# Layer 1 of the last batches behind layer 0 of the last batch, in a two-layer cross-attention kernel

## The reference

```python
x = x + _L0_xattn_ref(_layernorm(x), ctx_512, ...)   # causal self attention + cross attention, 16 heads of 16
x = x + _L0_ffn_ref(_layernorm(x), w1, b1, w2, b2)   # per-token int8 inputs, ternary weights, exact gelu
x = x + _L1_xattn_ref(_layernorm(x), ctx_512, ctx_512, ...)  # cross attention, 16 heads
x = x + _L1_ffn_ref(_layernorm(x), w1, b1, w2, b2)   # int8 with ONE scale over all batches
```

## Time and profile before

| | us |
|---|---|
| median of 3 runs | 1926.49 (1925.32 to 1931.07) |
| the profiled execution | 1921.53 |
| its span, first to last instruction | 1919.7 |
| PE busy in the span | 1685.9 |
| DVE busy | 1370.9 |
| ACT busy | 1156.6 |
| POOL busy | 659.1 |
| mean granted TensorE clock | 0.946 |

### The profile page before, as it was taken

The page is one execution under the profiler, slowest core; times in us unless marked ns, Lnnn a source line. Parts: engine busy times, 40 slices in busy tenths (PEclk is TensorE's granted clock), DMA queues, the critical chain, the costliest instruction groups (busy, mean ns, idle before and its releaser), DMA issues.

```text
span 1919.7 us, 29141 instructions
## 1 busy us (share of the span) xinstructions
PE 1685.9 (88%) x10052; PEld 732.4 (38%) x10064; DVE 1370.9 (71%) x2549; ACT 1156.6 (60%) x2178; POOL 659.1 (34%) x915
## 2 busy tenths in 40 slices
PE   4898889997999899998999899998999899678677
PEld 1344334423543344333542344333542354241236
DVE  6667767777687767777777758876777768638376
ACT  1374475566755585657655675567556676552597
POOL 3332523541454134522355044522354041140040
PEclk7898999999999999999999999999999999796998
DMA  7334313332242323331332324231333223014023
GB/s 198 88 104 127 89 34 95 83 93 69 60 110 63 85 67 93 84 97 56 94 87 73 86 56 115 75 90 56 95 84 86 59 56 96 0 52 147 23 88 111
DMA packets 106947, 159.49 MB, mean 83 GB/s; under 512 B 20656, under 2 KB 83248, under 8 KB 106800
## 3 DMA queue, kind: packets, MB, share of 16 engines
q1 hardware_dynamic: 101904, 156.43, 29.5%
...
## 4 chain that ended last, share of the span: by engine, by line
PE 54%; DVE 25%; ACT 10%; POOL 4%; issue 4%; DMA 1%; ACTq 0%; SPq 0%; DVEq 0%; POOLq 0%
DVE nmax L1222 13%; PE acc L1459 13%; PE mx L1424 11%; PE st L1445 9%; PE misc L1399 6%; PE misc L1371 4%; PE misc L1486 3%; PE misc L1411 3%; ACT probs L965 3%; ACT tail_h L1035 2%; DVE hid L1176 2%; ACT tail_h L1020 1%; ACT hid L1000 1%; PE misc L1513 1%; ACT hqT L924 1%
## 5 line engine op out<-in xcount | busy, mean ns | idle before, releaser
L1222 DVE TENSOR_REDUCE nmax<-mx 128x1 f32<-128x512 f32 (+2 forms) x1376 | 872.2, 673 | 318.4 <-PE mx L1424 189.5
L965 ACT ACTIVATE probs<-st 128x512 f32<-128x512 f32 (+3 forms) x1536 | 764.2, 549 | 410.4 <-PE st L1445 261.4
L1424 PE MATMUL mx<-stack 96*128 96x512 bf16 (+3 forms) x1536 | 550.8, 371 | 124.0 <-DVE nmax L1222 100.0
L1445 PE MATMUL st<-stack 99*128 99x512 bf16 (+3 forms) x1536 | 542.7, 366 | 28.8 <-ACT probs L965 27.3
L1424 PEld LDWEIGHTS mx<-stack 96*128 96x128 bf16 x1536 | 151.5, 99 | 355.1 <-DVE nmax L1222 281.3
L1445 PEld LDWEIGHTS st<-stack 99*128 99x128 bf16 x1536 | 149.6, 99 | 355.6 <-ACT probs L965 196.5
L844 POOL TENSOR_TENSOR parts<-qk,zero 128x512 bf16<-128x512 f32 x78 | 81.2, 1041 | 211.7 <-ACT qk L948 211.7
L1459 PE MATMUL acc<-probs,v_x 128*32 128x512 f32 x1024 | 145.9, 644 | 0.0
L1459 PE MATMUL acc<-probs,v_f 128*32 128x512 f32 x1024 | 140.0, 619 | 0.4 <-ACT probs L965 0.3
L856 POOL TENSOR_TENSOR nparts<-nmax,zero 128x16 bf16<-128x16 f32 x96 | 21.3, 222 | 287.0 <-DVE nmax L1222 287.0
L1448 PE MATMUL st<-mask_st,identb 128*128 128x128 bf16 x512 | 111.7, 221 | 0.0
...
## 6 DMA issues: line engine op xcount, KB each, us to landing
...
```

What stands on the lines that cost most here:

```text
L965: act.activation(probs[:, j % P_SLOTS, c, T - w:], st_bank(n, 4 * j + c)[:, 0:w], ACT.Exp, scale=SCALE).then_inc(exp_done, 1)
L1222: dve.tensor_reduce(nmax[:, ring, first:first + NT * (len(cs) - 1) + 1:NT], src, AX.X, ALU.max, negate=True).then_inc(mx_free, 1)
L1424: last = pe.matmul(o, stack[0:ROWS, r, 0, c, P * i:P * i + P], stack[0:ROWS, r, 1, c, 0:w], start=True, stop=not causal)
L1445: last = pe.matmul(o[:, 0:w], stack[0:AUG, r, 1, c, P * j:P * j + P], stack[0:AUG, r, 0, c, T - w:T], start=True, stop=not causal)
```

## The change

The same steps, 4374 in all, in another order from the start of x6_0 on:

```diff
-ORDER = [u for b in range(B + 1) for u in turn_units(b)]
+LATE = [(b, p) for b in (B - 2, B - 1) for p in "xs"] + [(b, "f") for b in (B - 3, B - 2, B - 1)]
+ORDER = [u for b in range(B - 2) for u in turn_units(b)] + [u for b, p in LATE for u in units(b, p)]
...
+def late_turns():
+    a, b, c = B - 3, B - 2, B - 1
+    keys_c, queries_c = project_qk(c, "f")[:2 * 4], project_qk(c, "f")[2 * 4:]
+    norm_c = [x for x in layer1_norm(c) if x != ("ctx_T", c, "C")]
+    f = units(c, "f")
+    first, second = ([("maxima", u, k) for k in banks_of(u)] for u in f[:2])
+    return [("load1", a), ("load0", c)] + \
+        slots(units(b, "x") + units(b, "s")[:1], [None] * 6 + [("y_T", a - 1, "C")] +
+              blend(ffn_main(a, [("residual", a - 1, "C"), ("v", b, "s")], layer1_last(a - 1)), tokens0(c) + project_qk(c, "x")) +
+              [("v", c, "x")], B) + \
+        slots(units(b, "s")[1:], [("load_mid", b)] + project_qk(c, "s") + layer1_norm(a) + [("v", a, "f"), None] + project_qk(a, "f"), B) + \
+        slots(units(c, "x")[:1], [None] * 6 + layer0_end(b) + [("load1", b)], B) + \
+        slots(units(c, "x")[1:] + units(c, "s"), ffn_norm(b) + ffn_main(b, [("v", c, "s")]) + [("load_mid", c)] +
+              layer1_norm(b) + [("v", b, "f"), None] + project_qk(b, "f"), B) + \
+        slots(units(a, "f")[:1], [None] * 6 + layer0_end(c) + [("load1", c)], B) + \
+        slots(units(a, "f")[1:], ffn_norm(c) + [("ctx_T", c, "C")] + blend(ffn_main(c, [("v", c, "f")]), keys_c), B - 1) + \
+        slots(units(b, "f")[:1], [None] * 3 + norm_c + queries_c, B - 1) + \
+        slots(units(b, "f")[1:2], [("stack", f[0])] + layer1_end(a) + [("stack", f[1])], B - 1) + \
+        slots(units(b, "f")[2:], first + [("negmax", f[0]), ("stack", f[2])] +
+              second[:9] + [("negmax_T", f[0])] + second[9:], B - 1) + \
+        slots(f[:1], [None] * 6 + layer1_end(b), B) + slots(f[1:], [], B) + close(f[-1]) + layer1_end(c)
```

As three batches now wait for layer 1 at once, their data get other buffers, and a few waits are added:

```diff
         def x1_of(s):
-            return y["s"] if last_batch(s) else x1
+            return {B - 2: ctx_all["A"][:, :].rearrange("p (t c) -> p t c", c=C), B - 1: y["s"]}.get(batch(s), x1)
         def xn_of(s, k):
-            return xn["A"] if k == "C" and last_batch(s) else xn[k]
+            return {("C", B - 2): xn["A"], ("E", B - 2): xn["A"], ("C", B - 1): xmid}.get((k, batch(s)), xn[k])
+        def y_of(s, p):
+            return {("f", B - 2): xn["A"], ("f", B - 1): y["x"]}.get((p, batch(s)), y[p])
+        def v_of(s, p):
+            return v_aug[{("f", B - 2): "x", ("f", B - 1): "s"}.get((p, batch(s)), p)]
+        def parts_of(b, w):
+            return qk_parts["x" + w[1] if (w[0], b) == ("f", B - 2) else w]
...
-            last_read("down", B - 1, NT - 1)
+            last_read("norm_T", B - 1, "C")
+            sp.wait_ge(peak, 2 * (B - 1))
             sp.wait_ge(stored, 32 * B)
...
+                if k == "C" and s.key[1] == B - 2:
+                    for m in range(KC):
+                        wait_misc_read(dve, s, m, ("norm_T", B - 1, "A"))
+                if k == "E" and last_batch(s):
+                    dve.wait_ge(stored, 32 * (B - 1))
...
+                    elif s.key[1] == B - 2:
+                        for m in range(KC):
+                            wait_misc_read(dve, s, 0, ("project", B - 1, "xk", m))
+                        for k in range(2):
+                            wait_misc_read(dve, s, k, ("v", B - 1, "x"))
...
                 if s.unit == (B - 1, "f", 0):
-                    dve.wait_ge(stored, 32 * B)
+                    dve.wait_ge(y_summed, B + 1)
```

More of the change, by code:

```diff
@@ L66, in turn_units, with units @@
     return layer0 + layer1
-ORDER = [u for b in range(B + 1) for u in turn_units(b)]
+def units(b, p):
+    return [(b, p, g) for g in range(NU)]
+LATE = [(b, p) for b in (B - 2, B - 1) for p in "xs"] + [(b, "f") for b in (B - 3, B - 2, B - 1)]
+ORDER = [u for b in range(B - 2) for u in turn_units(b)] + [u for b, p in LATE for u in units(b, p)]
 AT = {u: n for n, u in enumerate(ORDER)}
@@ L252, in turn @@
             slots(us[5:8], [("v", 1, "x"), ("load_mid", 0)] + weights([2, 3]) + project_qk(1, "s"), 1)
-    more = b + 1 < B
-    loads = [("load1", b - 1)] + ([("load0", b + 1)] if more else [])
+    loads = [("load1", b - 1), ("load0", b + 1)]
     if b == 1:
@@ L259, in turn @@
         start = slots(us[:5], [None] * 6 + [("y_T", b - 2, "C")] +
-                      ffn_main(b - 1, [("residual", b - 2, "C"), ("v", b, "s")], layer1_last(b - 2)) + layer1_start(b - 1), b + more)
-    if not more:
-        return loads + start + slots(us[5:6], [("load_mid", b)], b) + slots(us[6:8], [], b) + \
-            slots(us[8:9], [None] * 6 + layer0_end(b), b) + \
-            slots(us[9:12], layer0_ffn(b) + [("load1", b)] + layer1_norm(b) + project_qk(b, "f"), b)
-    return loads + start + \
-        slots(us[5:6], [("load_mid", b)] + (tokens0(b + 1) if more else []), b + more) + \
-        slots(us[6:8], project(b + 1, "x") if more else [], b + more) + \
-        slots(us[8:9], [None] * 6 + layer0_end(b), b + more) + \
-        slots(us[9:12], blend(ffn_norm(b), project_qk(b + 1, "s")), b + more)
+                      ffn_main(b - 1, [("residual", b - 2, "C"), ("v", b, "s")], layer1_last(b - 2)) + layer1_start(b - 1), b + 1)
@@ new lines, in turn @@
+    return loads + start + \
+        slots(us[5:6], [("load_mid", b)] + tokens0(b + 1), b + 1) + \
+        slots(us[6:8], project(b + 1, "x"), b + 1) + \
+        slots(us[8:9], [None] * 6 + layer0_end(b), b + 1) + \
+        slots(us[9:12], blend(ffn_norm(b), project_qk(b + 1, "s")), b + 1)
+def late_turns():
[19 more added lines that the diff above has]
+        slots(f[:1], [None] * 6 + layer1_end(b), B) + slots(f[1:], [], B) + close(f[-1]) + layer1_end(c)
@@ L275 @@
     warm_up(FIRST)[3:] + [("consts_rest", 0)]
-AFTER = close((B - 2, "f", NU - 1)) + warm_up(turn_units(B))[:3] + layer1_end(B - 2) + [("v", B - 1, "f")] + \
-    warm_up(turn_units(B))[3:] + slots(turn_units(B), [], B, True) + close((B - 1, "f", NU - 1)) + layer1_end(B - 1)
 TURNS = [[s for s in steps if s] for steps in
-         [BEFORE + turn(0) + turn(1)] + [turn(b) for b in range(2, B - 1)] + [turn(B - 1) + AFTER]]
+         [BEFORE + turn(0) + turn(1)] + [turn(b) for b in range(2, B - 2)] + [late_turns()]]
 RING_USES = {
@@ L306, in shifted @@
     return (s[0], later) + s[2:]
-for t in range(1, B - 3):
-    assert [shifted(s) for s in TURNS[t]] == TURNS[t + 1], "the loop's turns differ"
 RING_PER_TURN = {r: START[TURNS[2][0]][r] - START[TURNS[1][0]][r] for r in RING_USES}
@@ L1458, in values @@
                 for c in range(HU):
-                    last = pe.matmul(acc[32 * c:32 * c + 32, T - w:T], v_aug[p][:, j, HU * g + c, :],
+                    last = pe.matmul(acc[32 * c:32 * c + 32, T - w:T], v_of(s, p)[:, j, HU * g + c, :],
                                      probs[:, j % P_SLOTS, c, T - w:T], start=j == 0, stop=j == NT - 1)
```

24 lines of the change are left out of this document (14 added, 10 removed).

## The result

The changed kernel takes **1910.55 us** (median of 4, 1909.33 to 1911.45) where the kernel before took 1925.9 beside it: ratio 0.9916, 95% interval [0.9897, 0.9935]. The interval leaves out 1, so it is faster, by 15 us or 0.8%. The forecast was 1886.0 with a range of 1872 to 1905: the sign was right, the size was not, and the range didn't reach the result. The profiled execution took 1909.82 us with a span of 1908.0.

The account below looks back on a forecast made before the run. It took TensorE's work to bound a steady turn. Pieces priced mostly in TensorE time summed to 458.7 us for the 499.2 us reordered stretch, 40.5 less, giving 1886.0 us for the median, range 1872 to 1905.

Parts of the forecast that it names:

- The bubble: From the start of f6_3 to f7_0, 61.8 us with TensorE busy 45.7, because f7 needs all of batch 7's layer 0.
- (b): Rival at batch 7's layer-1 start: keys and queries still late, the 12.4 us chain comes back bare; 1898 us, chance 0.05.
- (c): Rival where projections bunch (s6_1, s6_3, s7_3): maxima splits queue on GpSimd and TensorE waits, 53 us; 1939 us, chance 0.03.
- (d): Rival: idle time only moves and nothing is gained, 1.6 us more in each of 25 units; chance 0.03.
- The loads for the last FFN: Issued in f7_1, beside the maxima rows of f7_2 and f7_3: bounds 0 to 3 us, taken as 0.
- The pieces x6_0 to s6_3: Cross-attention and causal units of batch 6: 99.9 us for x6_0 to s6_0, 51.0 for s6_1 to s6_3.
- `layer1_end` at 4.7 us: End of layer 1, in f6_1 and f7_0: priced in TensorE time from turn 6 at 4.7 us each.
- The quantisation and the gelu, 12.5 us each time: Layer-0 FFN in x7_1 to x7_3 and f5_1 to f5_3: quantisation 4.5 us, gelu 8.0, beyond their matmuls.
- rival (a): Late gelu blocks cost what f6_1 and f6_2 did, 19.8 us instead of 12.5, twice, 14.6 more; 1901 us, chance 0.14.
- x7_0 and f5_0: First units of batch 7's cross-attention and batch 5's layer 1, each priced at 16.8 us as f5_0 before.
- second way of counting: Check on the reordered stretch: TensorE's 432.2 us busy less 18 us of lower clock, over 0.924, gives 448 us.
- TensorE busy over 90% of the stretch: Sign of a right forecast: TensorE busy over 90% from 1270 to the start of f7_1.

Follow-up runs that it names:

- experiment 9: The changed kernel once more, with no edit, as a base for later runs: median 1911.53 us, ratio 0.9922 to the kernel before.
- Experiments 3: Changed kernel with 3.6 us more TensorE work in batch 5's layer-1 end and 3.6 us more VectorE work in batch 6's: 1916.37 us.
- experiment 4: Changed kernel with layer 1's last statistics, norm, peak and store of batches 5 and 6 moved behind the start of f7_2: 1902.49 us, ratio 0.9871.
- experiment 11: Changed kernel with layer 1's last part moved, GpSimd's addition held until after quantisation, and scale and quantisation spread among maxima: 1894.66 us, ratio 0.9832.
- after: The changed kernel as first measured and profiled, against the kernel before: median 1910.55 us, profiled execution 1909.82, ratio 0.9916.
- experiment 5: Changed kernel with GpSimd's row addition of batches 6 and 7 waiting until VectorE has made the quantised copy: 1907.78 us.
- Experiment 2: Changed kernel with each split of the layer-1 projections made four list entries of one VectorE operation, maxima between: 1909.14 us.

## Why the prediction was wrong, point by point

**Right.** The bubble is gone, and the rivals that spoke against it didn't come true. (b) f7_0's stack was no constraint: its maxima lie in f6_2, which at 14.1 us is a nearly bare unit. (c) GpSimd's queue: s6_1 to s6_3 took 50.3 where I had 51.0, so four splits of projections in a row cost nothing. (d) is out as well, with 19.7 us gained in the stretch. The loads for the last FFN beside the rows of f7 cost nothing: f7_2 took 10.7 in both kernels. The pieces x6_0 to s6_3, where TensorE is the bound, held within 1.5 us.

**The step that failed, and the largest term of the miss: `layer1_end` at 4.7 us.** I priced it, as every moved step, in TensorE time from turn 6. It costs 4.7 on TensorE and some 4 us on VectorE, and in a unit of only its own maxima these are paid one after the other. It cost 9.3 in f6_1 (22.7 for 13.4) and 9.1 over f7_0 and f7_1 (35.9 for 26.8), 9.0 us more than in my sum for the two, and 10.1 in experiment 9. Experiments 3 and 4 show it, by adding to the chain and by taking it away: without the VectorE part the units give back 8.0 of the 9.0, and the kernel takes 1902.49. The row was in front of me: a bare unit, f7_1, keeps VectorE busy for 10.62 of 13.40 us, and I had used it for TensorE's length only. In turn 6 units of 17 us hid such a chain.

**The quantisation and the gelu, 12.5 us each time.** By my pieces, x7_1 to x7_3 paid 9.0 for both and f5_1 to f5_3 22.1; rival (a) had 19.8 for each. The late gelu of batch 6 was not dear: x7_2 and x7_3 took 36.3, only 1.5 more than their work. (f5_2 took 24.6 to 26.2 us at a clock of 0.86 or 0.87 in all 13 executions, as its row in 11 shows; no experiment aimed at it, and what the gelu of batch 7 costs there is open.) What was mis-sized is the quantisation. I took 4.5 for each, with 1.0 for the collision of `tok_xam` with GpSimd. It was a full 2.1 us in f5_1 (2.27 for 0.17) and 0.5 in x7_1 (L1185 took 0.68 for 0.16), and in f5_1 it stands in a chain that made a pause of 6.11 us, during which the clock fell. I costed the collision as VectorE time, and not the pause of TensorE that the whole chain makes, nor the lower clock: 17.1 us of it in after, 10.2 in experiment 9 with the same pause. The collision by itself (experiment 5) is worth 0.5 to 3.1 us of f5_1 to f5_3, the collision and the unbroken chain together (11) 4.6 by experiment 9 and 7.2 by after. With both gone, f5_1 to f5_3 still pay 14.9 for quantisation and gelu where I had 12.5.

The rule of the Trainium skill that I had weighed (GPSIMD Engine Reference, Specifications: GpSimd's SBUF interfaces are shared with VectorE) names VectorE instructions with two SBUF inputs, and two rows here bear it out: 1.68 for 0.16 and 2.70 for 0.69. The third, 2.27 for 0.17, is an operation with one SBUF input; it would fall under the rule if it ran in a 2-port perf mode, which no run here shows. As each held up operation ended with the addition or just behind it, the price is the rest of GpSimd's instruction, whatever the size of VectorE's.

**Two edits that I had at nothing.** x7_0 and f5_0 are f5_0 of the kernel before by their steps (16.8), and took 19.7 and 20.9: the last split of the layer-1 queries now ends in them, 2.2 us of VectorE ahead of their maxima. I had read the split's end only as the start of f7's stack. Experiment 2 gives back 5.2 of the 7.0 us (of 6.1, 4.4 by experiment 9).

**The check by the clock.** I took the granted clock to rise to 0.97 once the bubble is gone, and my second way of counting used 98% of full speed. It rose from 0.92 to 0.95; in experiment 11, with the pauses shortened, to 0.97. I had treated the lower clock as a property of the bubble, but it comes up in many units, and not in step with their pauses: at the start of x7_0 the same pause of 1.73 us came with 3.4 us at the 1.2 GHz level in after, 6.8 in experiment 4 and none in experiment 9. Of my other signs, TensorE busy over 90% of the stretch failed (422.2 of 479.5, 88%), and f7_1 started at 1753.7 and not near 1729.

**Luck.** The net miss hides larger ones. The late gelu of batch 6 and the downs behind it (x7_2 to s7_1) took 9.8 us less than priced; without that the forecast would have been some 34 us too low. Part of it fits the theory: the maxima that VectorE computes in these four units are those of causal units, 10 or 11 operations and 6.4 to 7.0 us in each, where f5_1 to f5_3 have 16 and 10.9, and the 13.4 us at which I priced x7_2 and x7_3 are those of a unit with the longer ones. No experiment tried it.

**The range** was too narrow because all its terms were lengths of units in which the moved steps had more room, and because both ways of counting were counts of TensorE time: they agreed with each other and shared the error.
